# In the last attention round, the queries are made ahead of the expert sums, and the round's fill table is written anew

## The chip, the cores and the metric

The kernel runs on one core of a Trainium2 chip. The metric is the device time of one launch in microseconds (us): the median before is 1268.89 us over 3 runs (1267.88 to 1271.37). The engines are TensorE (PE in the profile, PEld its weight loads), VectorE (DVE), ScalarE (ACT), GpSimd (POOL) and SyncE (SP), which only issues DMAs here.

## The reference

Sixteen images become 49 tokens each, a class token and 128 text tokens are added, and the 178 tokens by 192 channels go through two attention layers and a mixture of four experts.

```
h = tokens(x)                                   # patch conv, wavelet branch, 3 depthwise convs, layernorm
h = concatenate([h, txt], axis=1)               # 16 x 178 x 192
h = h + attn(layernorm(h))                      # 12 heads of 16, own token masked, softmax, projection
h = h + ffn(layernorm(h))
...
def ffn(src):
    logits = gamma * zscore_last(Q @ K.T * scale)      # z-score over the 178 keys, per row
    attn = softmax(logits) @ V @ Wo.T + bo
    x = layernorm(src + attn) * g + b
    top-2 of softmax(x @ Wg.T + bg) over E = 4 experts -> combine
    y[e] = relu(x @ W1[e] + b1[e]) @ W2[e] + b2[e]     # 192 -> 768 -> 192
    return layernorm(x + sum_e combine[e] * y[e]) * g + b
```

## The kernel before, in words

The images are handled in 8 pairs. A pair passes three stages: attention 0 (the masked one), attention 1 (the one with z-scored logits) and the experts. The stages of different pairs run beside each other in rounds, `one_round(eng, a, b, nxt, m, fill)`: in one round attention 0 works on pair `a`, attention 1 on pair `b`, pair `nxt` is loaded and projected, and the experts work on pair `m`. Every engine has its own written-out program for a round (`pe_round`, `act_round`, `dve_round`, `sp_round`, `pool_round`), and the engines are tied together by semaphores. An engine works strictly in its written order: while it waits for one semaphore, nothing behind that wait can start.

The change is about the last round that has attention, `one_round(eng, None, PAIRS - 1, None, PAIRS - 2, FILL_B7)`: `a` and `nxt` are None, attention 1 works on pair 7 and the experts on pair 6. One more round follows with the experts of pair 7 alone.

Attention 1 in that round goes so. TensorE transposes the normed input (L749), projects queries (L757), keys (L757 again) and values (L765). VectorE first centres the input (`xbar`, L1268 to L1274), then closes the pair before it (`last.finish()`: the output layernorm of pair 5, L1166 to L726), splits the keys into three bf16 parts (L1185 to L1188, `ks`) and adds the value bias (L1195, L1199). From key Gram matrices (L878, L889, L895, L901, the last one called the ss sums here) and four ScalarE activations (L1086 to L1091) comes the factor `rem` of each query. VectorE multiplies the queries by it and splits them (`query`: L1303, L1185 to L1188, `qs`). SyncE stores `qs` to DRAM (L1527, `scr_q`) and loads it back in stacked form in six parts (L1534, `qst`); TensorE waits for all of them before the max pass (`pe_max_pass`: logits L792 and L798; VectorE takes the row maxima, `mx`, L1317). The maxima are split (L1323 to L1329), transposed (L825), cast on ScalarE (`mrows`, L1045) and sent by DMA into `qst` (L1545). Then comes the exp pass (`pe_exp_pass`: logits again, exponentials L1055, products with the values L851), the normalisation (L860, L1338, L1339), the projection (L866, L765) and the layernorm whose result is transposed at L966 for the experts of pair 7.

The expert work of pair 6 is cut into 50 steps, numbered 0 to 49. An even step `2u` is a group of five matmuls of 370 columns (L646, first layer of unit `u`); ScalarE's relu (`hid`, L681) follows. An odd step `2u+1` is the second layer of unit `u-1` (L668; printed as x6 in the profile, since each of three matmuls is two instructions). Four times VectorE adds an expert's sum to `acc` (`expert`, L696): it belongs to steps 13, 25, 37 and 48, and waits until TensorE has finished them; TensorE waits for the sum before it starts the next expert's second layer.

Where these steps stand among the attention work is set by the fill table: `moe.point("ss")` runs as many steps as the table has under "ss", and the three engines TensorE, ScalarE and VectorE call the same points in the same order. What the points have not used runs at `moe.rest()`. The names of points: "start", "norm", "query", "key", "value", "kc", "g", "u", "ss" in the front; ("max", 1) with a number for each of the six head pairs of the max pass; ("split", 1) after it; ("rows", 1) before the exp pass; ("exp", 1) with six numbers; ("out", 1), ("turn", 1), ("back", 1) in the output part. Points with a 0 are of attention 0 and are not called here.

Of the kernel before, what the change touches and what calls it, by code (L numbers as in the profile page):

```python
# [100 lines left out]
    "next query": 2,  # L101
}
FILL_B7 = {
    "start": 4, "norm": 1, "query": 3, "key": 4, "value": 0, "kc": 2, "g": 0, "u": 2, "ss": 14,
    ("max", 0): (0, 0, 0, 1, 1, 0), ("split", 0): 0, ("rows", 0): 0, ("exp", 0): (0, 0, 0, 0, 0, 0), ("out", 0): 1,
    ("max", 1): (0, 0, 0, 0, 0, 0), ("split", 1): 1, ("turn", 0): 1, ("back", 0): 2, ("rows", 1): 4,
    ("exp", 1): (1, 2, 0, 0, 0, 2), ("out", 1): 1, ("turn", 1): 2, ("back", 1): 0, "next turn": 0, "next norm": 3,
    "next query": 2,
}


# [15 lines left out]
def build(nc, a):  # L127
    ctx = ExitStack()
    with ctx:
        def sb(name, shape, dt=F32):  # L130
            return ctx.enter_context(nc.sbuf_tensor(name, shape, dt))
# [26 lines left out]
        rows = sb("rows", [128, NROW, D])  # L158
# [410 lines left out]
        def at(n, per, k):  # L569

            return n * per + k
# [167 lines left out]
        def moe_of(cls, eng, m, fill):  # L739
            return NoMoe() if m is None else cls(eng, m, fill)  # L740
# [163 lines left out]
        def pe_round(pe, a, b, nxt, m, fill):  # L904


            moe = moe_of(MoePe, pe, m, fill)
# [35 lines left out]
                pe.wait_ge(S["m_rows", 1], at(b, 1, 1))  # L943
            if a is not None:
                pe_out(pe, 0, a, moe)
                moe.point(("rows", 1))
                pe.wait_ge(S["pr_read", 0], at(a, 1, 1))
            if b is not None:
                pe_exp_pass(pe, 1, b, moe)
# [21 lines left out]
            if b is not None:  # L971
# [3 lines left out]
                for i in range(3):  # L975
                    o = 2 * E * i
                    for k, (x, plane) in enumerate(((x2T_hi, 0), (x2T_lo, 0), (x2T_hi, 1), (x2T_lo, 1))):
                        w = gate_b[:] if plane else gate_a[:].rearrange("p c e -> p (c e)")
                        ins = nc.tensor.matmul(PS[:, 2, o:o + (E if plane else 2 * E)], tile_cols(x, plane, i), w,  # L979
                                               start=(k == 0), stop=(k == 3), skip_group_check=True)  # L980
# [30 lines left out]
        def act_turn_in(act, s, r):  # L1011
            act.wait_ge(S["xT_psum", s], at(r, 1, 1))
            first = front(s, r)[0]
            src = PS[0:HC, first:first + 2, 0:XW]
            nc.scalar.copy(xT[s][:], src).then_inc(S["xT_ready", s], 1)  # L1015
# [53 lines left out]
        def act_out(act, s, r, moe):  # L1069
            moe.point(("turn", s))  # L1070
            act.wait_ge(S["oc_psum", s], at(r, 1, 1))
            nc.scalar.copy(oT[:], PS[0:HC, 0:2, 0:XW]).then_inc(S["oc_ready", s], 1)
            moe.point(("back", s))
# [20 lines left out]
        def act_round(act, a, b, nxt, m, fill):  # L1094
            moe = moe_of(MoeAct, act, m, fill)
            moe.point("start")
            if b is not None:
                act_turn_in(act, 1, b)
                moe.point("norm")
                act_query(act, 1, b)  # L1100
                moe.point("query")
                act_key(act, 1, b, a)
                moe.point("key")
                moe.point("value")
                act_deviation(act, b, moe)
                moe.point("ss")
            if a is not None:
                for u in range(HH):
                    moe.point(("max", 0), u)
                moe.point(("split", 0))  # L1110
                act_max_rows(act, 0, a)
                moe.point(("rows", 0))
                act_exp_pass(act, 0, a, moe)
                moe.point(("out", 0))
            if b is not None:
                for u in range(HH):
                    moe.point(("max", 1), u)
                moe.point(("split", 1))
                act_max_rows(act, 1, b)
            if a is not None:  # L1120
                act_out(act, 0, a, moe)
                moe.point(("rows", 1))
            if b is not None:
                act_exp_pass(act, 1, b, moe)
                moe.point(("out", 1))
            if b is not None:
                act_out(act, 1, b, moe)
            if nxt is not None:
                act_turn_in(act, 0, nxt)
                moe.point("next turn")  # L1130
                moe.point("next norm")
                act_query(act, 0, nxt)
                moe.point("next query")
                act_key(act, 0, nxt, b)
            moe.rest()
            if b is not None:
                act.wait_ge(S["x2T_psum"], at(b, 1, 1))
                nc.scalar.copy(x2T_hi[:], PS[:, 2:4, 0:XW]).then_inc(S["x2T_ready"], 1)
                act.wait_ge(S["gl_ready"], at(b, 1, 1))
                nc.scalar.activation(gl[:], gl[:], ACT.Exp).then_inc(S["ge_ready"], 1)  # L1140
# [241 lines left out]
        def dve_round(dve, a, b, nxt, m, fill):  # L1382
            moe = moe_of(MoeDve, dve, m, fill)
            last = moe_of(MoeDve, dve, None if m is None or isinstance(m, int) and m == 0 else m - 1, fill)
            moe.point("start")
            if b is not None:
                query = dve_front1(dve, b, a, moe, last)
                moe.point("ss")
            else:
                last.finish()  # L1390
            if a is not None:
                dve_max_pass(dve, 0, a, moe)
                moe.point(("split", 0))
            if b is not None:
                query(a)
            if a is not None:
                moe.point(("rows", 0))
# [6 lines left out]
            if a is not None:  # L1404
                dve_out(dve, 0, a, moe)
                norm1 = dve_norm1(dve, a)
                moe.point(("rows", 1))
            if b is not None:
                for u in range(HH):
                    moe.point(("exp", 1), u)  # L1410
# [333 lines left out]
```

## Time and profile before

| | |
|---|---|
| median of 3 runs | 1268.89 us |
| profiled execution | 1264.83 us, its span 1263.0 us |
| PE busy | 86% of the span |
| DVE, ACT, POOL busy | 54%, 32%, 4% |
| share of the last chain: PE, DVE, ACT, DMA | 64%, 13%, 4%, 2% |
| last attention round (first L646 of pair 6 to L966) | about 1088.4 to 1195.7 us of the span |

The times come from one profiled execution. Times of day in the rows are microseconds from the start of the span; a duration follows; a bracket tells how long the engine had been idle before and what ended that. Matmuls are pipelined, so listed durations of neighbours overlap; the price of a group is the distance between starts, which the chain of waits gives directly. "issue" in a bracket means that the profile names no releaser.

### The profile page before, as it was taken

Reading aid. Unit: us, or ns where it says so; the run is one execution under the profiler, and the core shown is the slowest. Engines: PE = TensorE matmul, PEld = TensorE weight load, DVE = VectorE, ACT = ScalarE, POOL = GpSimd, SP = SyncE. Lnnn points to the kernel's source line nnn. Section 1 sums busy time; section 2 is a strip of 40 time slices with the busy share of each in tenths; the row PEclk is TensorE's granted clock in tenths of the full one; section 3 lists DMA queues with packets and bytes.
Section 4 is the critical chain, followed back from the end, with each engine's and each line's share of the span. In section 5 each row is a group of like instructions: output and inputs, shape, how many; then the busy total and the mean of one; then the engine's idle time right before and its main releaser. Section 6 shows DMA issues by size and latency. Waiting matters only on the chain.

```text
span 1263.0 us, 18670 instructions
## 1 busy us (share of the span) xinstructions
PE 1090.2 (86%) x7404; PEld 798.9 (63%) x7404; DVE 679.8 (54%) x1874; ACT 398.4 (32%) x905; POOL 55.1 (4%) x90
## 2 busy tenths in 40 slices
PE   7798747786789999999999999999999999885895
PEld 4343424553467677767866785787578667773795
DVE  3367677344465457646746565576547643633332
ACT  1222222213322343334343334333343234221321
POOL 6011100000000000000000000000000000000000
PEclk9898867756689899989998999999899989895998
DMA  9000052422032204220530152033204220021000
GB/s 302 0 1 0 7 156 60 68 43 44 8 73 55 45 8 91 59 34 4 110 68 10 32 104 44 9 63 73 44 8 85 52 44 2 4 62 29 1 10 9
DMA packets 38478, 60.74 MB, mean 48 GB/s; under 512 B 5060, under 2 KB 30264, under 8 KB 37944
## 3 DMA queue, kind: packets, MB, share of 16 engines
q1 hardware_dynamic: 36112, 56.84, 21.0%
q10 hardware_dynamic: 2280, 2.72, 0.8%
q8 instruction: 58, 0.95, 0.3%
q14 instruction: 28, 0.23, 0.1%
HBM read 42.76 MB, written 16.34 MB: 47 GB/s over the span
## 4 chain that ended last, share of the span: by engine, by line
PE 64%; DVE 13%; ACT 4%; issue 3%; DMA 2%; SPq 1%; POOL 0%; DVEq 0%; ACTq 0%; POOLq 0%
PE PS L668 14%; PE PS L646 12%; PE PS L757 7%; DVE mx L1317 6%; PE PS L851 5%; PE PS L765 5%; PE PS L792 5%; PE PS L798 3%; PE PS L807 2%; PE PS L860 2%; PE PS L889 1%; DMA qst<-mrows 1%; PE PS L979 1%; ACT probs L1055 1%; DVE acc L696 1%
## 5 line engine op out<-in xcount | busy, mean ns | idle before, releaser
L668 PE MATMUL PS<-w,hid 128*128 128x192 f32 x1152 | 230.8, 338 | 3.0 <-DVE acc L696 1.8
L681 ACT ACTIVATE hid<-PS,b 128x370 f32<-128x370 f32 x192 | 109.1, 569 | 329.2 <-PE PS L646 327.5
L668 PEld LDWEIGHTS PS<-w,hid 128*128 128x128 f32 x1152 | 197.8, 196 | 12.8 <-issue 4.7
L1317 DVE TENSOR_REDUCE mx<-PS 128x2 f32<-128x356 f32 x288 | 128.4, 519 | 130.1 <-PE PS L792 102.5
L1055 ACT ACTIVATE probs<-PS 128x356 f32<-128x356 f32 x288 | 111.9, 484 | 30.2 <-PE PS L792 20.7
L646 PE MATMUL PS<-x2T_hi,w_hi 128*128 128x370 f32 x192 | 91.6, 477 | 0.0
L792 PE MATMUL PS<-kst,qst 96*128 96x178 bf16 x384 | 69.7, 278 | 17.5 <-issue 12.3
L757 PE MATMUL PS<-xT,w_at 96*96 96x370 f32 x192 | 78.3, 559 | 7.2 <-ACT xT L1015 3.5
L807 PE MATMUL PS<-masks,ident_bf 128*128 128x256 bf16 (+1 forms) x288 | 76.6, 266 | 0.0
L851 PE MATMUL PS<-probs,va 128*17 128x178 f32 x1536 | 69.2, 321 | 6.4 <-ACT probs L1055 6.4
L792 PE MATMUL PS<-qst,kst 99*128 99x178 bf16 x384 | 56.7, 251 | 17.8 <-DMA qst<-mrows 12.9
L646 PE MATMUL PS<-x2T_hi,w_lo 128*128 128x370 f32 x192 | 66.0, 344 | 0.0
L646 PE MATMUL PS<-x2T_hi,w_rest 128*128 128x370 f32 x192 | 65.9, 343 | 0.0
L646 PE MATMUL PS<-x2T_lo,w_hi 128*128 128x370 f32 x192 | 65.8, 343 | 0.0
L646 PE MATMUL PS<-x2T_lo,w_rest 128*128 128x370 f32 x192 | 65.5, 341 | 0.0
L757 PEld LDWEIGHTS PS<-xT,w_at 96*96 96x96 f32 x192 | 34.7, 189 | 41.1 <-issue 11.3
L1338 DVE RECIPROCAL rs<-PS 128x36 f32<-128x36 f32 x16 | 6.1, 382 | 100.1 <-PE PS L860 100.1
L792 PEld LDWEIGHTS PS<-kst,qst 96*128 96x128 bf16 x384 | 25.8, 104 | 53.4 <-DVE mx L1317 31.9
L851 PEld LDWEIGHTS PS<-probs,va 128*17 128x17 f32 x1536 | 40.5, 98 | 23.8 <-ACT probs L1055 9.3
L792 PEld LDWEIGHTS PS<-qst,kst 99*128 99x128 bf16 x384 | 28.1, 100 | 43.3 <-issue 26.1
L696 DVE SCALAR_TENSOR_TENSOR acc<-PS,comb,acc 128x192 f32<-128x192 f32 x72 | 25.5, 410 | 54.7 <-PE PS L668 54.7
L375 DVE SCALAR_TENSOR_TENSOR dwo<-pad_l,chan,dwo 96x441 f32<-96x441 f32 x48 | 38.1, 793 | 26.7 <-ACT cw L299 25.2
(226 smaller groups left out, 1723.8 us busy)
## 6 DMA issues: line engine op xcount, KB each, us to landing
qst<-scr_q SPq DMA_DIRECT2D x96, 144.0 KB, 4.8
scr_q<-qs SPq DMA_DIRECT2D x16, 432.0 KB, 3.3
scr_k<-ks SPq DMA_DIRECT2D x16, 432.0 KB, 3.7
kst<-scr_k SPq DMA_DIRECT2D x16, 432.0 KB, 5.0
kst<-scr_k SPq DMA_DIRECT2D x16, 288.0 KB, 5.9
cols<-in_x_cols SPq DMA_DIRECT2D x6, 392.0 KB, 13.4
w<-in_w SPq DMA_DIRECT2D x1, 2304.0 KB, 26.7
kst<-scr_k SPq DMA_DIRECT2D x16, 144.0 KB, 6.3
```

The source lines that it names most:

```text
L375: ch.link(nc.vector.scalar_tensor_tensor(out=out, in0=image_rows(PAD_OF[r][:, 0, :], tap_offset(t), n), scalar=col(C_DW + 18 * r + t), in1 ...
L646: ins = nc.tensor.matmul(PS[:, 4 + u % 2, 0:XN], w[:, f], x[:, plane, 0:XN], start=(k == 0), stop=(k == 4))
L668: ins = nc.tensor.matmul(tile_psum((6, 7), i), hid[u % 2][:, 128 * i:128 * i + 128], w2[:, u, :], start=(j == 0 and i != 1), stop=(j == FT ...
L681: nc.scalar.activation(hid[u % 2][:, 0:XN], PS[:, 4 + u % 2, 0:XN], ACT.Relu, bias=b1[:, u:u + 1]).then_inc(S["h_ready"], 1)
L696: ins = nc.vector.scalar_tensor_tensor(out=acc[:, i, :], in0=tile_psum((6, 7), i), scalar=comb[:, i, e:e + 1], in1=(acc if e else x2)[:, i ...
L757: ins = nc.tensor.matmul(PS[0:HC, banks[m], 0:XN], w_at[:, w, k, HC * m:HC * m + HC], x[:, k, 0:XN], start=(k == 0), stop=(k == 1))
L765: ins = nc.tensor.matmul(tile_psum(banks, i), tile_cols(x, k, i), w_at[:, w, k, :], start=(k == 0), stop=(k == 1))
L792: ins = nc.tensor.matmul(PS[:, bank, T * b:T * b + T], still[0:rows_, h, TP * b:TP * b + NTXT], move[0:rows_, h, TP * b:TP * b + T], start ...
L807: ins = nc.tensor.matmul(own, ident_bf[:], m.rearrange("p (b j) -> p b j", b=2), start=False, stop=True, skip_group_check=True)
L851: ins = nc.tensor.matmul(PS[32 * q:32 * q + VW, 3, T * b:T * b + T], va[s][:, 2 * i + b, h, :], pr, start=(i == 0), stop=(i == 1), skip_gr ...
L1055: nc.scalar.activation(probs[:, u % PROB_UNITS, bank, :], PS[:, bank, 0:T2], ACT.Exp)\
L1317: nc.vector.tensor_reduce(out, PS[:, g, 0:T2].rearrange("p (b j) -> p b j", b=2), AX.X, ALU.max)\
```

## The change

The fill table of this round, `FILL_B7`, gets new numbers. Summed over the points that are called, they give 39 steps before the rest in both kernels, but placed otherwise: before, 30 steps stand ahead of the max pass, none in it, 1 after it, none at ("rows", 1), 5 in the exp pass, 1 at "out", 2 at "turn", none at "back"; in the changed kernel 22, 4, 3, 4, 3, 0, 2 and 1. Of the 22, five stand in the front (three at "query", two at "key") and 17 at "ss".

The point ("rows", 1) is now called in rounds without `a` too. And in a round without `a`, VectorE calls `query` ahead of the point "ss" and no longer behind it. The other attention rounds have an `a` and keep their order; in the round after the last attention round the point ("rows", 1) runs one step of the table FILL that ran at the rest before, in the same order.

```diff
 FILL_B7 = {
-    "start": 4, "norm": 1, "query": 3, "key": 4, "value": 0, "kc": 2, "g": 0, "u": 2, "ss": 14,
-    ("max", 0): (0, 0, 0, 1, 1, 0), ("split", 0): 0, ("rows", 0): 0, ("exp", 0): (0, 0, 0, 0, 0, 0), ("out", 0): 1,
-    ("max", 1): (0, 0, 0, 0, 0, 0), ("split", 1): 1, ("turn", 0): 1, ("back", 0): 2, ("rows", 1): 4,
-    ("exp", 1): (1, 2, 0, 0, 0, 2), ("out", 1): 1, ("turn", 1): 2, ("back", 1): 0, "next turn": 0, "next norm": 3,
-    "next query": 2,
+    "start": 0, "norm": 0, "query": 3, "key": 2, "value": 0, "kc": 0, "g": 0, "u": 0, "ss": 17,
+    ("max", 0): (0, 0, 0, 0, 0, 0), ("split", 0): 0, ("rows", 0): 0, ("exp", 0): (0, 0, 0, 0, 0, 0), ("out", 0): 0,
+    ("max", 1): (0, 1, 1, 1, 1, 0), ("split", 1): 3, ("turn", 0): 0, ("back", 0): 0, ("rows", 1): 4,
+    ("exp", 1): (0, 1, 0, 1, 0, 1), ("out", 1): 0, ("turn", 1): 2, ("back", 1): 1, "next turn": 0, "next norm": 0,
+    "next query": 0,
 }
@@ pe_round @@
             if a is not None:
                 pe_out(pe, 0, a, moe)
-                moe.point(("rows", 1))
+            moe.point(("rows", 1))
+            if a is not None:
                 pe.wait_ge(S["pr_read", 0], at(a, 1, 1))
@@ act_round @@
                 act_out(act, 0, a, moe)
-                moe.point(("rows", 1))
+            moe.point(("rows", 1))
@@ dve_round @@
                 query = dve_front1(dve, b, a, moe, last)
+                if a is None:
+                    query(a)
                 moe.point("ss")
...
-            if b is not None:
+            if b is not None and a is not None:
                 query(a)
...
                 norm1 = dve_norm1(dve, a)
-                moe.point(("rows", 1))
+            moe.point(("rows", 1))
```

On VectorE, in the last attention round before, the expert sums (`acc`) of steps 13 and 25 stand ahead of the queries (`q`, `qs`), and the 18 row maxima (`mx`) stand in one piece:

```order
L696 SCALAR_TENSOR_TENSOR acc<-PS,comb,x_wide 128x192 x3
L1290 TENSOR_TENSOR probs<-PS,same_head 96x192 x2
L1297 TENSOR_TENSOR rem<-PS,q 96x4x178
L696 SCALAR_TENSOR_TENSOR acc<-PS,comb,acc 128x192 x3
L1303 SCALAR_TENSOR_TENSOR q<-q,chan,rem 96x4x178
L1185 CAST qs<-q 96x2x2x178
L1186 TENSOR_TENSOR rem<-q,qs 96x4x178
L1187 CAST qs<-rem 96x2x2x178
L1188 TENSOR_TENSOR qs<-rem,qs 96x2x2x178
L1317 TENSOR_REDUCE mx<-PS 128x2 x18
```

The same place of VectorE in the changed kernel, where these lines are numbered one higher:

```order
L1291 TENSOR_TENSOR probs<-PS,same_head 96x192 x2
L1298 TENSOR_TENSOR rem<-PS,q 96x4x178
L1304 SCALAR_TENSOR_TENSOR q<-q,chan,rem 96x4x178
L1186 CAST qs<-q 96x2x2x178
L1187 TENSOR_TENSOR rem<-q,qs 96x4x178
L1188 CAST qs<-rem 96x2x2x178
L1189 TENSOR_TENSOR qs<-rem,qs 96x2x2x178
L696 SCALAR_TENSOR_TENSOR acc<-PS,comb,x_wide 128x192 x3
L1318 TENSOR_REDUCE mx<-PS 128x2 x15
L696 SCALAR_TENSOR_TENSOR acc<-PS,comb,acc 128x192 x3
L1318 TENSOR_REDUCE mx<-PS 128x2 x3
```

Both sums moved behind the queries: the first stands before the maxima, the second between the fifteenth and the sixteenth of them.

On TensorE, at the end of the max pass of the same round before: the last logits (L792, L798), one step, and the transposes of the maxima (L825).

```order
L798 MATMUL PS<-kst,qst 64x178 x4
L792 MATMUL PS<-kst,qst 128x178 x4
L798 MATMUL PS<-kst,qst 64x178 x4
L646 MATMUL PS<-x2T_hi,w_hi 128x370
L646 MATMUL PS<-x2T_hi,w_lo 128x370
L646 MATMUL PS<-x2T_lo,w_hi 128x370
L646 MATMUL PS<-x2T_hi,w_rest 128x370
L646 MATMUL PS<-x2T_lo,w_rest 128x370
L825 MATMUL PS<-ident,mpart 36x128 x3
```

TensorE in the max pass of the changed kernel, from the second head pair's logits on:

```order
L792 MATMUL PS<-kst,qst 128x178 x4
L798 MATMUL PS<-kst,qst 64x178 x4
L646 MATMUL PS<-x2T_hi,w_hi 128x370
L646 MATMUL PS<-x2T_hi,w_lo 128x370
L646 MATMUL PS<-x2T_lo,w_hi 128x370
L646 MATMUL PS<-x2T_hi,w_rest 128x370
L646 MATMUL PS<-x2T_lo,w_rest 128x370
L792 MATMUL PS<-kst,qst 128x178 x4
L798 MATMUL PS<-kst,qst 64x178 x4
L668 MATMUL PS<-w,hid 128x192 x3
L792 MATMUL PS<-kst,qst 128x178 x4
```

A step now follows the logits of each of the head pairs 1 to 4; three more stand before L825 and four between L825 and the exp pass.

## Rows read from the trace of the kernel before

**Rows 1.** The page, busy time of TensorE: busy us (share), instructions.

```profile
PE 1090.2 (86%) x7404; PEld 798.9 (63%) x7404; DVE 679.8 (54%) x1874; ACT 398.4 (32%) x905; POOL 55.1 (4%) x90
```

**Rows 2.** Timeline of TensorE, 1145 to 1196 us: start, duration, instruction, idle before.

```profile
1145.00 0.75 PE L792 MATMUL PS<-kst,qst 96*128 96x178 bf16 x4 [12.26 <-issue]
...
1155.57 0.80 PE L825 MATMUL PS<-ident,mpart 128*36 128x128 f32 x3 [1.05 <-DVE mpart L1326]
1160.74 0.75 PE L792 MATMUL PS<-qst,kst 99*128 99x178 bf16 x4 [4.37 <-DMA qst<-mrows]
...
1161.86 2.29 PE L668 MATMUL PS<-w,hid 128*128 128x192 f32 x6
...
1181.53 2.22 PE L765 MATMUL PS<-w_at,oT 96*128 96x192 f32 x12 [0.88 <-ACT oT L1072]
...
1195.69 0.88 PE L966 MATMUL PS<-ident,x_wide 128*128 128x128 f32 x6
```

**Rows 3.** Timeline of VectorE, 1114 to 1153 us.

```profile
1114.96 0.90 DVE L1297 TENSOR_TENSOR rem<-PS,q 96x712 f32<-96x712 f32 x1 [1.54 <-PE PS L895]
1128.49 1.07 DVE L696 SCALAR_TENSOR_TENSOR acc<-PS,comb,acc 128x192 f32<-128x192 f32 x3 [12.64 <-PE PS L668]
1129.59 0.96 DVE L1303 SCALAR_TENSOR_TENSOR q<-q,chan,rem 96x712 f32<-96x712 f32 x1
...
1132.64 0.90 DVE L1188 TENSOR_TENSOR qs<-rem,qs 96x712 bf16<-96x712 f32 x1
1145.50 7.93 DVE L1317 TENSOR_REDUCE mx<-PS 128x2 f32<-128x356 f32 x18 [11.96 <-PE PS L792]
```

**Rows 4.** Timeline of ScalarE, the last activation before the queries.

```profile
1120.44 0.80 ACT L1091 ACTIVATE rem<-rem 96x712 f32<-96x712 f32 x1
```

**Rows 5.** Timeline of SyncE, the queries' store and loads.

```profile
1133.62 0.30 SPq L1527 DMA_DIRECT2D scr_q<-qs  x1
1136.91 2.63 SPq L1534 DMA_DIRECT2D qst<-scr_q  x6
```

**Rows 6.** Timeline of TensorE in the round's front, 1092 to 1122 us.

```profile
1092.98 0.82 PE L749 MATMUL PS<-ident,xn 128*96 128x128 f32 x6
...
1094.68 2.73 PE L757 MATMUL PS<-xT,w_at 96*96 96x370 f32 x8
...
1116.59 1.36 PE L901 MATMUL PS<-rem,same_head 96*96 96x356 f32 x4
...
1121.75 1.24 PE L668 MATMUL PS<-w,hid 128*128 128x192 f32 x6 [1.12 <-ACT hid L681]
```

**Rows 7.** Timeline of VectorE in the round's front, 1094 to 1110 us.

```profile
1094.66 0.68 DVE L1268 TENSOR_REDUCE xbar<-xT 96x4 f32<-96x512 f32 x1 [2.79 <-ACT xT L1015]
...
1103.11 0.76 DVE L726 TENSOR_TENSOR fin<-fin,h_fin 128x576 f32<-128x576 f32 x1
...
1108.84 0.71 DVE L1199 TENSOR_TENSOR va<-PS,rows 50x192 f32<-50x192 f32 x2
```

**Rows 8.** Chain of waits, two steps and a head pair's logits: start, us, what.

```profile
1125.66 0.98 PE PS L668 x6
1126.63 0.84 PE PS L646 x5
...
1172.08 0.41 PE PS L792 x4
1172.49 0.27 PE PS L798 x4
```

**Rows 9.** Stretches of 2 us, TensorE: length, PE busy (instructions), granted clock, DMA share, GB/s.

```profile
1030.00:1032.00 2.00, 1.90 (x11) 0.73 0.00 0
...
1084.00:1086.00 2.00, 0.12 (x1) 0.88 0.00 0
...
1120.00:1122.00 2.00, 0.88 (x5) 1.00 0.00 0
...
1164.00:1166.00 2.00, 2.00 (x17) 0.99 0.00 0
```

## The prediction

> **What bounds the kernel now.** I read the page's busy times first: TensorE is busy for 86% of the span [rows 1], so what can be won is its idle time, and what matters is where that lies. The chain of waits and TensorE's timeline of the last attention round show it. Ahead of the max pass TensorE stands still for 12.26 us; 1.05 us ahead of the transposes of the maxima, 4.37 us ahead of the exp pass [rows 2]. Then I followed the 12.26 us back. The six stacked query loads were issued from 1136.91, after a store at 1133.62 [rows 5], which waited for the last piece of the query split at 1132.64 + 0.90 = 1133.54 [rows 3]. The factor that the queries need was ready at 1120.44 + 0.80 = 1121.24 [rows 4], but VectorE took the queries up only at 1129.59: in its order an expert sum stood before them, for which it had waited 12.64 us [rows 3]. So 8.35 us of the standstill are order and not work. Also, after the long waits TensorE ran at half its rate: a second-layer step that costs 0.98 on the chain [rows 8] is listed with 2.29 us at 1161.86 [rows 2], against 1.24 us at 1121.75 [rows 6].
>
> **The change part by part.** All instructions stay; only places change. I place the changed round on the clock of the profiled execution.
>
> *The front.* Eight steps leave it (13 before "ss" to 5). One pair of steps costs 0.98 + 0.84 = 1.82 us on the chain [rows 8], so TensorE has 7.3 us less to do there. But VectorE then sets the pace. Before the input's sums at 1094.66 it had waited 2.79 us for the input, so it was free from 1091.87 [rows 7]. TensorE now transposes right after the gate matmuls and the gate's read, at about 1089.1 (the timeline has the last gate matmul at 1088.2 and the read ended at 1089.0), 0.8 us at full clock and up to 1.6 at half [rows 6], and ScalarE's copy takes 0.8, so VectorE starts at 1091.9, 2.76 earlier. Its work from 1094.66 to the end of `fin` at 1103.87 (9.2 us) moves as a block to end at 1101.1. The query and key projections cost 2.5 us each at full clock (a row of eight is listed with 2.73 [rows 6]); the first falls into the slow stretch after the gate, some 4.8 us, to 1096; two relu groups to 1097.7, keys to 1100.2, ScalarE's copy to 1101.1. So both releasers of the key split meet at 1101.1. A split takes 2.95 us (the queries' from 1130.59 to 1133.54, behind L1303 [rows 3]), the value bias 1.2 (its last piece of 0.71 in [rows 7], 0.5 for the first): 1105.3. From there before: the Gram product (1.87), mask (0.77), `u` product (1.45), `rem` (1.0), ss sums (1.3) make 6.4 us without steps between: ss sums end at 1111.8. Before they ended at 1116.59 + 1.36 = 1117.95 [rows 6]. **Gain 6.2 us.** Ends: if the clock stays low, see the slow rival (the end moves to 1124.7, a loss of 6.8); nothing lets it be better than 8.2 us, TensorE's removed steps plus the two waits of the block.
>
> *The queries.* ScalarE's four activations take 3.28 us (1117.96 to 1121.24), then VectorE starts after 0.05 and not after 8.35. Work and trip stay: 3.95 us for queries and split [rows 3], 11.46 us from the end of the split to the first logits at 1145.00 [rows 2, 5]. 1111.8 + 3.28 + 0.05 + 3.95 + 11.46 = 1130.5. **Gain 8.3 us.** SyncE has nothing in front of this store: key store and loads are now some 2.6 us earlier too. TensorE's 17 steps beside it: three run (2.8 us), then it waits for ScalarE, whose relus stand behind the four activations, as it waited 1.12 us before [rows 6]; fourteen take 7 x 1.82 = 12.7, plus 0.4 for the first expert sum: finished at 1128.7. So it waits about 1.8 us instead of 12.26. The expert sum behind the queries costs nothing, since VectorE is free from 1119.1 and the sum is asked for at about 1122.
>
> *Max pass to exp pass.* Before 15.74 us (1145.00 to 1160.74 [rows 2]) with one step inside; now eleven. VectorE needs 7.93 / 18 = 0.44 us for a maximum [rows 3]. TensorE needs 0.41 + 0.27 = 0.68 for the logits of a head pair [rows 8] and 0.84 to 0.98 for the step, 1.6 together, against 1.32 on VectorE: TensorE becomes the bound. Two head pairs, held by VectorE, to 1.9; four steps 3.7 and three more logits 2.0: 7.6. Now the second expert sum comes in between (1.1), then the last three maxima (1.3), the split of the maxima (2.0), 0.15: the transposes start 12.1 us after the pass, where it was 10.57. The three steps (2.8 us) hide behind this. From the transposes to the exp pass 5.17 us before, 4.9 with the transposes at full clock; the four steps (3.7) lie inside the DMA. Sum 17.1. **Loss 1.4 us.** Bounds: 15.4 if the step and the sum hid wholly, 25 at half clock (first rival).
>
> *Exp pass to L966.* Before 34.95 us (1160.74 to 1195.69 [rows 2]). Two steps fewer: 1.9. Full clock at its start saves the 1.25 us of the slow step and 0.5 of the logits. The step at "back" fills the wait of 0.88 ahead of L765 [rows 2]. The step missing at "out" opens 0.6. **Gain 4.0 us**, between 1.9 (only the steps) and 4.6.
>
> Sum: 6.2 + 8.3 - 1.4 + 4.0 = 17.1 us. The round of pair 7's experts that follows keeps its order and its length. I take 0.6 us off for hand-overs between engines that I rounded away in the two denser stages: 16.5 us. The profiled execution took 1264.83 us (span 1263.0) and would take 1248.3; the median of the runs is 1268.89, 0.3% above it. I take the 16.5 us from the median: 1252.4.
>
> **The clock.** The granted clock has two levels here. It fell at about 1085.5, in the stretch in which TensorE, after a wait, was busy for 0.12 of 2 us (a mean of 0.88 is half clock for the last 0.5 us), and it stayed at 1.00 where it was busy for 0.88 of 2 us between full work; it also fell, to a mean of 0.73, at 1030.9, where TensorE did logits in step with VectorE without steps between them [rows 9]. After the exp pass had begun at 1160.74, it came back at 1164.0 [rows 2, 9]. The new waits of the front are 1.0, 0.8 and 1.0 us, the one ahead of the max pass 1.8, with full work on both sides: nearer to the row that kept the clock. The Trainium skill has a rule against this (TensorE: Matmul & The Clock Gate, "A second HAM failure mode: psum-queue depth-cycling"): frequent micro-idles while a kernel cycles through PSUM banks make the clock switch back and forth between its levels. The fall at 1030.9 agrees with it. By that rule the max pass would still run cold, and the result would be the first rival's; by the row at 1120 it would run warm.
>
> **The rivals.**
> First: the clock falls in the 1.8 us or in the first logits. For: 1.8 us is near the waits before 1085.5, and the max pass of the round before fell so. Against: there, no step stood in the first three head pairs; now one follows the second. Price: four steps and the logits at half rate take 13.0 us where 7.6 stood, the four steps ahead of the exp pass 7 where 4.4 are covered: 8 us. Gain 8.5, 1260.4.
> Second: the front keeps its length, because VectorE's closing of the last pair and the slow clock decide it and not the removed steps. For: VectorE has 9.2 + 2.95 + 1.2 us to do in a row. Against: its wait of 2.79 us is plainly in the rows. Then 6.2 us are missing: gain 10.3, 1258.6.
> Third, slower: without the steps at "start" and "norm", TensorE's front is short work between waits, and the clock that fell at 1085.5 does not come back before the exp pass. Then front and steps cost double: ss sums at 1124.7, 17 steps of 1.54 to 1.94 us to 1155, the max pass as in the first rival and with three slow steps behind it, exp pass at 1182.3 instead of 1147.6. That is 34.7 us against the 17.1: 17.6 slower, 1286.5. It decides once the low clock lasts beyond about half of this stretch, some way into the 17 steps. Against: the query and key projections alone are solid work longer than that which brought it back at 1164.0.
> Fourth: no change. This needs the third to hold for just half of the stretch, or the expert steps to be the bound throughout; TensorE's standstill of 12.26 speaks against the latter.
>
> **How the numbers follow.** The forecast 0.62 (its own range 1250.3 to 1255.5, from the ends of the terms), first rival 0.17, second 0.10, third 0.04, no change 0.03; 0.04 for a larger gain, where all hand-overs turn out shorter. The range 1249.8 to 1261 takes in the first two rivals. A difference of about 0.3%, 3.8 us, is what a measurement of this kernel can tell from none: faster 0.93, within it 0.03, slower 0.04.
>
> **What would show it.** Measured from the last gate matmul: VectorE's first query instruction within 0.1 us of the end of ScalarE's last activation; store to first logits 11 to 12 us; TensorE's idle ahead of the max pass 1 to 3 us in place of 12.26; clock 1.00 from the first logits to the exp pass; idle ahead of the exp pass below 1.5 us; L966 about 90 us after the last gate matmul where it was 107. It is wrong if the clock is at half in the max pass (then by the first rival), if the key split starts later than 13 us after the last gate matmul (second), or if the wait ahead of the max pass stays above 5 us.

## The result, and the profile after

The changed kernel takes 1255.76 us in the median of 6 runs (1251.88 to 1258.30), the kernel before 1268.65 (1263.73 to 1271.37, 6 runs). The ratio is 0.9905, 95% interval 0.9885 to 0.9925: 0.75% to 1.15% faster. Timed again later, the same kernel had 0.9916 (0.9892 to 0.9941). The forecast of 1252.4 lay 3.4 us too low: within the stated range of 1249.8 to 1261, but just outside the forecast's own range of 1250.3 to 1255.5.

The profiled execution took 1251.88 us, its span is 1250.1 us. Its page reads for TensorE, columns as in [rows 1]:

```profile
PE 1086.6 (87%) x7404; PEld 795.4 (64%) x7404; DVE 680.3 (54%) x1874; ACT 398.3 (32%) x905; POOL 55.4 (4%) x90
```

The same number of instructions, and 12.9 us less span: 9.3 us of it are idle time of TensorE, 3.6 us busy time (1090.2 to 1086.6). TensorE's timeline of the last attention round, which answers to [rows 2]:

```profile
1089.14 4.88 PE L757 MATMUL PS<-xT,w_at 96*96 96x370 f32 x8 [0.88 <-ACT xT L1016]
...
1108.87 1.44 PE L901 MATMUL PS<-rem,same_head 96*96 96x356 f32 x4 [0.99 <-DVE rem L1298]
...
1129.28 0.47 PE L792 MATMUL PS<-kst,qst 96*128 96x178 bf16 x4 [2.22 <-issue]
...
1134.49 2.29 PE L668 MATMUL PS<-w,hid 128*128 128x192 f32 x6
...
1145.38 0.49 PE L825 MATMUL PS<-ident,mpart 128*36 128x128 f32 x3 [1.23 <-DVE mpart L1327]
1146.48 1.24 PE L668 MATMUL PS<-w,hid 128*128 128x192 f32 x6 [0.61 <-ACT mrows L1047]
...
1150.24 0.47 PE L792 MATMUL PS<-qst,kst 99*128 99x178 bf16 x4
```

The wait ahead of the max pass is 2.22 us in place of 12.26, and ahead of the exp pass there is none in place of 4.37. But between them stands a step of 2.29 us at 1134.49, the mark of the half clock.

VectorE's timeline answers to [rows 3]:

```profile
1107.92 0.90 DVE L1298 TENSOR_TENSOR rem<-PS,q 96x712 f32<-96x712 f32 x1 [1.54 <-PE PS L895]
1113.63 0.96 DVE L1304 SCALAR_TENSOR_TENSOR q<-q,chan,rem 96x712 f32<-96x712 f32 x1 [4.82 <-ACT rem L1092]
...
1116.68 0.90 DVE L1189 TENSOR_TENSOR qs<-rem,qs 96x712 bf16<-96x712 f32 x1
1119.14 1.07 DVE L696 SCALAR_TENSOR_TENSOR acc<-PS,comb,x_wide 128x192 f32<-128x192 f32 x3 [1.56 <-PE PS L668]
1129.70 2.71 DVE L1318 TENSOR_REDUCE mx<-PS 128x2 f32<-128x356 f32 x6 [9.50 <-PE PS L792]
1133.87 1.40 DVE L1318 TENSOR_REDUCE mx<-PS 128x2 f32<-128x356 f32 x3 [1.46 <-PE PS L792]
1137.12 1.40 DVE L1318 TENSOR_REDUCE mx<-PS 128x2 f32<-128x356 f32 x3 [1.85 <-PE PS L792]
```

The queries now wait for ScalarE alone and start as its last activation ends (1113.60). The maxima, one piece of 7.93 us before, are broken by waits of 1.46 and 1.85 us for TensorE. The stretches of 2 us around the max pass (columns as in [rows 9]):

```profile
1128.00:1130.00 2.00, 0.72 (x8) 1.00 0.00 0
1130.00:1132.00 2.00, 1.52 (x11) 0.77 0.00 0
1132.00:1134.00 2.00, 2.00 (x9) 0.50 0.00 0
...
1136.00:1138.00 2.00, 2.00 (x12) 0.52 0.00 0
1138.00:1140.00 2.00, 2.00 (x16) 1.00 0.04 8
```

The clock fell to its lower level (1.2 of 2.4 GHz) at about 1131.1, within the first logits, and was back at 1138.0.

For comparing kernels I cut the round at fixed instructions. Each number below is a difference of starts (ends for the last gate matmul and the ss sums) in one profiled execution of each kernel, in us. "Front" runs from the last gate matmul to the end of the ss sums, "trip" from there to the first logits of the max pass, then to L825, to the exp pass, and to L966; "tail" is from L966 to the end of the span. The labels are those of the experiments below. "ss 18" is a kernel with 18 steps at the point "ss"; a "spin" is a group of added matmuls whose result nobody uses and which only keep TensorE busy.

| | front | trip (TensorE's wait at its end) | to L825 | to exp pass | to L966 | sum | tail |
|---|---|---|---|---|---|---|---|
| before | 29.4 | 27.05 (12.26) | 10.57 | 5.17 | 34.95 | 107.1 | 67.3 |
| changed | 24.05 | 18.97 (2.22) | 16.10 | 4.86 | 31.60 | 95.6 | 68.3 |
| e11, changed again | 24.06 | 18.92 (2.17) | 16.13 | 4.87 | 31.61 | 95.6 | 68.2 |
| e1, queries only | 30.2 | 19.46 (4.67) | 10.51 | 5.17 | 35.65 | 101.0 | 68.2 |
| e2, table only | 24.0 | 25.60 (8.92) | 16.23 | 4.86 | 31.60 | 102.3 | 68.1 |
| e12, front only | 28.3 | 31.80 (12.93) | 10.58 | 5.17 | 35.97 | 111.8 | 68.3 |
| e8, start 4 | 29.4 | 18.74 (3.64) | 16.05 | 4.89 | 31.61 | 100.7 | 68.3 |
| e6, rows 0 | 24.0 | 18.94 (2.25) | 16.11 | 4.86 | 36.97 | 100.9 | 67.0 |
| e4, ss 18 | 24.1 | 19.42 (1.81) | 15.42 | 5.02 | 31.61 | 95.5 | 68.2 |
| e5, ss 19 | 24.0 | 19.01 (0.51) | 13.86 | 6.46 | 31.57 | 94.9 | 68.4 |
| e3, spin | 24.9 | 18.77 (0.0) | 13.18 | 4.86 | 31.60 | 93.3 | 68.2 |
| e9, two spins | 24.9 | 18.74 (0.0) | 13.18 | 4.86 | 31.60 | 93.3 | 65.6 |
| e10, pass spins | 28.9 | 18.87 (0.0) | 12.44 | 4.87 | 31.61 | 96.7 | 64.7 |
| e7, ss 19, gate spins | 27.85 | 18.84 (0.0) | 14.80 | 6.49 | 31.61 | 99.6 | 64.5 |

Of the 12.9 us between the two spans, 11.5 lie in the round. The last gate matmul itself came 2.3 us earlier in the changed kernel's profile (1086.26 against 1088.57), though no instruction before it has changed: in the profiled executions of the kernels that are alike up to there it lies anywhere from 1079.5 to 1092.8. The tail took 1.0 us back, though its instructions are those of before: the clock stood at 0.50 for 6.8 us there before and for 10.2 us in the changed kernel, and e1 and e12, whose tails are those of before too, have 68.2 and 68.3. So the round is the better measure of a single cause, and the timed medians of the whole. The round has a spread of its own: the front of e1 and the stretch from exp pass to L966 of e1 and e12 have the instructions of before, and took 0.8, 0.7 and 1.0 us longer.

### The profile page after: what moved, and what is told of

Its sections match the earlier page's. It is cut to its first block, busy times and chain, and to the rows that moved or that the text cites. A ratio compares the mean times of both kernels' runs of the same rounds, so it can differ in the third digit from the quotient of the medians.

```text
span 1250.1 us, 18671 instructions
## 1 busy us (share of the span) xinstructions
PE 1086.6 (87%) x7404; PEld 795.4 (64%) x7404; DVE 680.3 (54%) x1874; ACT 398.3 (32%) x905; POOL 55.4 (4%) x90
## 4 chain that ended last, share of the span: by engine, by line
PE 64%; DVE 14%; ACT 4%; DMA 2%; issue 2%; SPq 1%; POOL 0%; DVEq 0%; ACTq 0%; POOLq 0%
PE PS L668 15%; PE PS L646 12%; PE PS L757 7%; DVE mx L1318 6%; PE PS L851 5%; PE PS L765 5%; PE PS L792 5%; PE PS L798 3%; PE PS L807 2%; PE PS L860 2%; PE PS L889 1%; DMA qst<-mrows 1%; ACT probs L1056 1%; PE PS L980 1%; DVE acc L696 1%
## 5 line engine op out<-in xcount | busy, mean ns | idle before, releaser
L792 PE MATMUL PS<-kst,qst 96*128 96x178 bf16 x384 | 67.8, 273 | 8.8 <-issue 2.2
L792 PE MATMUL PS<-qst,kst 99*128 99x178 bf16 x384 | 56.0, 248 | 13.7 <-DMA qst<-mrows 8.6
L792 PEld LDWEIGHTS PS<-kst,qst 96*128 96x128 bf16 x384 | 26.2, 104 | 42.8 <-DVE mx L1318 30.0
L792 PEld LDWEIGHTS PS<-qst,kst 99*128 99x128 bf16 x384 | 27.4, 99 | 38.9 <-issue 21.0
```

Source lines behind the costliest of these rows:

```text
L792: ins = nc.tensor.matmul(PS[:, bank, T * b:T * b + T], still[0:rows_, h, TP * b:TP * b + NTXT], move[0:rows_, h, TP * b:TP * b + T], start ...
```

## The experiments

Each kernel was timed beside the kernel before. Given are medians, and the ratio to before with its 95% interval; what is said of a stretch comes from one profiled execution of each kernel.

**e1, only the queries ahead.** Fill table and point ("rows", 1) as before.

```diff
                 query = dve_front1(dve, b, a, moe, last)
+                if a is None:
+                    query(a)
                 moe.point("ss")
...
-            if b is not None:
+            if b is not None and a is not None:
                 query(a)
```

> Only VectorE's query call is moved ahead of the point ss; fill table and the point (rows, 1) as before. Theory (order on VectorE holds the trip through DRAM, one for one): the queries start 8.3 us earlier, the first logits 8.3 us earlier (TensorE's wait ahead of the max pass about 4 us in place of 12.26), the rest of the round as before: 7.5 to 9 us faster than before, about 1260.5. Rival (the table is what pays, the trip only moves the wait): under 4 us faster, and the wait turns up again ahead of the exp pass.

1259.61 us (12 runs), ratio 0.9960 (0.9935 to 0.9986). The trip is 7.6 us shorter, not 8.3: from the end of the split to the first logits it took 12.2 us here against 11.5 before. The front was 0.8 us longer, with the clock back at its upper level 5.4 us after the last gate matmul where it was 3.8 before, and the stretch behind the exp pass's start 0.7. The round is 6.2 us shorter: the theory's mechanism, a little under its numbers. The rival had the wait turn up again ahead of the exp pass; it is 4.37 us there, as before, so that part is refuted. The rival's size (under 4 us) lies inside the interval of the timed runs, which is 1.8 to 8.2 us. VectorE:

```profile
1124.36 0.96 DVE L1303 SCALAR_TENSOR_TENSOR q<-q,chan,rem 96x712 f32<-96x712 f32 x1 [5.42 <-ACT rem L1091]
...
1131.58 1.07 DVE L696 SCALAR_TENSOR_TENSOR acc<-PS,comb,acc 128x192 f32<-128x192 f32 x3 [3.27 <-PE PS L668]
```

The queries wait for ScalarE alone; TensorE waits 0.41 us for the expert sum behind them, as it did before.

**e2, only the table and the point ("rows", 1).** The queries stand behind "ss" as before.

> The new fill table with the point (rows, 1), but the queries behind the point ss as before. By the theory the front keeps its 5.3 us, but the queries now wait for the first expert sum, which in the changed kernel began 5.5 us after the queries did: they start 6.6 us later than in the changed kernel, TensorE waits about 9 us ahead of the max pass, and the low clock then lasts through the whole max pass with its steps inside. 1 to 5 us faster than before, 8 to 12 slower than the changed kernel. The rival (table pays alone) wants at least 9 us faster than before.

1262.52 us (12 runs), ratio 0.9979 (0.9953 to 1.0004). The round is 102.3 us, 4.8 less than before and 6.7 more than in the changed kernel. The trip is 6.6 us longer than there, as forecast; the round is less so than the 8 to 12 us expected. The rival (at least 9 us faster than before) falls, since the interval ends at 6 us; that the table alone gains at all is not resolved by the timed runs. The low clock lasted 13.6 us, from the long wait until 8.8 us into the pass, and not through the whole of it. Since the stretch to L825 is 16.23, the same as the changed kernel's, the long wait cost nothing beyond itself.

**e12, the front alone.** The kernel before with the five steps of "start" and "norm" put at "ss".

```diff
-    "start": 4, "norm": 1, "query": 3, "key": 4, "value": 0, "kc": 2, "g": 0, "u": 2, "ss": 14,
+    "start": 0, "norm": 0, "query": 3, "key": 4, "value": 0, "kc": 2, "g": 0, "u": 2, "ss": 19,
```

> The kernel before with the five steps of start and norm moved to ss (14 to 19), nothing else: the queries still stand behind the expert sum of step 25. Theory: the front shrinks by 5.3 us as in the changed kernel, but step 25 is now the 15th of ss and no longer the 10th, 4.6 us later behind the front's end, so the queries start only about 1 us earlier: 0 to 2 us faster than before. Rival (what leaves the front is gained wherever it goes): 4 to 6 us faster.

1269.19 us (12 runs), ratio 1.0043 (1.0016 to 1.0069): slower, which neither expectation had. The front shrank by 1.1 us and not by 5.3. Its clock was back at the upper level only 9.9 us after the last gate matmul, where it was 3.8 us before; how much of the missing 4.2 us that explains was not measured. The trip grew by 4.75, which was forecast. VectorE shows the sum of step 25 in front of the queries and what the wait for it costs:

```profile
1110.72 1.07 DVE L696 SCALAR_TENSOR_TENSOR acc<-PS,comb,x_wide 128x192 f32<-128x192 f32 x3 [5.01 <-PE PS L668]
1122.42 1.07 DVE L696 SCALAR_TENSOR_TENSOR acc<-PS,comb,acc 128x192 f32<-128x192 f32 x3 [10.63 <-PE PS L668]
1123.53 0.96 DVE L1303 SCALAR_TENSOR_TENSOR q<-q,chan,rem 96x712 f32<-96x712 f32 x1
```

So moving steps from the front to "ss" costs on the trip what it saves in the front, as long as the queries stand behind the sum of step 25. In e2, where only the sum of step 13 stood ahead of them, the round still gained 4.8 us.

**e8, four steps back at start.** "start": 4, "ss": 13, else the changed kernel.

> The changed kernel with four of the 17 steps of ss back at start. By theory the input is transposed about 4 us later, VectorE's block starts 2.9 us later, and the front is 27 us again in place of 24.05; TensorE then waits about 6 us ahead of the max pass, and the clock is low in all of it. 3 to 7 us slower than the changed kernel. Rival (the front is bound by TensorE's sum of work, so it only matters that 8 steps have left it): the front grows by all of 3.6 to 5 us. Second rival (the start was no bound): under 1 us slower.

1257.72 us (8 runs), ratio 0.9925 (0.9900 to 0.9950). The front is 29.4 us, 5.3 more than in the changed kernel and the whole of its gain; that is the first rival's size. The theory's cause gives part of it: VectorE's block started 3.7 us later after the last gate matmul (forecast 2.9), its key split 3.1 us later. The other 2.3 us came behind the key split, where the clock fell in the thin work of the front (stretches of 2 us):

```profile
1106.00:1108.00 2.00, 1.04 (x11) 1.00 0.46 112
1108.00:1110.00 2.00, 1.38 (x12) 0.90 0.37 109
1110.00:1112.00 2.00, 1.91 (x7) 0.50 0.87 194
```

In the timed runs the loss against the changed kernel is not resolved (intervals overlapping).

**e6, no steps at ("rows", 1).**

```diff
-    ... ("rows", 1): 4,
-    ("exp", 1): (0, 1, 0, 1, 0, 1), ...
+    ... ("rows", 1): 0,
+    ("exp", 1): (1, 2, 1, 1, 1, 1), ...
```

> The changed kernel without the four steps at (rows, 1); they run in the exp pass instead (1, 2, 1, 1, 1, 1). If those steps are hidden by the DMA that brings the maxima, TensorE stands 4.3 us idle again ahead of the exp pass and the exp pass grows by 3.7: 3.3 to 5 us slower than the changed kernel, more (up to 7) if the clock falls in that wait. Rival (the exp pass has room for four more steps beside ScalarE's exponentials): under 1.5 us slower.

1259.23 us (10 runs), ratio 0.9942 (0.9922 to 0.9962). The wait is back and the time to the exp pass does not change at all:

```profile
1148.01 0.49 PE L825 MATMUL PS<-ident,mpart 128*36 128x128 f32 x3 [1.19 <-DVE mpart L1327]
1152.87 0.75 PE L792 MATMUL PS<-qst,kst 99*128 99x178 bf16 x4 [4.36 <-DMA qst<-mrows]
```

The stretch behind grew from 31.60 to 36.97: four steps (3.7 us) and 1.7 more, with the clock at 0.50 when the exp pass began. The round is 5.3 us longer. The four steps at ("rows", 1) were hidden wholly.

**e3, TensorE kept busy ahead of the pass.** The added matmuls write a PSUM bank that is free then; the result does not use them.

```diff
                 moe.point("ss")
                 pe.wait_ge(S["ss_read"], at(b, 1, 1))
+                if a is None:
+                    for _ in range(12):
+                        nc.tensor.matmul(PS[:, 3, 0:XN], w1_hi[:, 0:128], x2T_hi[:, 0, 0:XN], start=True, stop=True, ...)
```

> The changed kernel with 12 added matmuls of 370 columns (0.17 us each, 2.1 us, into a PSUM bank that nobody reads then) where TensorE waited 2.22 us ahead of the max pass. If that wait is what lets the clock fall at 1131, the granted clock stays 1.00 through the max pass, the stretch from first logits to exp pass shrinks from 20.96 to about 17 us, and the kernel is 3 to 4.5 us faster than the changed one (14.5 to 17 faster than before). Rival (the short waits between logits make it fall, whatever stood before): the clock falls at the same place and the kernel is within 1 us of the changed one. Second rival: the added work is on the path, 0 to 1 us slower.

1253.20 us (7 runs), ratio 0.9900 (0.9862 to 0.9938). TensorE, then its clock, around the first logits:

```profile
1129.10 2.37 PE L813 MATMUL PS<-x2T_hi,w_hi 128*128 128x370 f32 x12
1131.42 0.48 PE L792 MATMUL PS<-kst,qst 96*128 96x178 bf16 x4
```

```profile
1129.00:1131.00 2.00, 2.00 (x14) 1.00 0.37 46
1131.00:1133.00 2.00, 1.63 (x15) 1.00 0.00 0
1133.00:1135.00 2.00, 1.90 (x17) 1.00 0.00 0
```

The clock stays at its upper level, and the stretch to L825 takes 13.18 us in place of 16.10: 2.9 us is what the fall had cost. In the round it is 2.3 us, less than the 3 to 4.5 forecast, since its front was 0.85 us longer: the clock came back 8.8 us after the last gate matmul, and 7.2 in the changed kernel. In the timed median the gain over the changed kernel is not resolved (0.9900 against 0.9905 and 0.9916, intervals overlapping).

**e4 and e5, real steps in that wait.** 18 steps at "ss" and ("max", 1) (0, 1, 1, 1, 0, 0); 19 and (0, 0, 0, 1, 1, 0).

> The changed kernel with one step more at the point ss (18) and one less in the max pass (head pair 4 has none). The step (0.85 us) runs in the wait of 2.22 us ahead of the max pass and leaves it. If the clock stays up by it, 3 to 5 us faster than the changed kernel; if the clock falls as before, about 1 to 1.5 us faster, since a step less runs at the low clock; if the max pass is bound by VectorE, no difference.

> The changed kernel with 19 steps at ss and two in the max pass (head pairs 3 and 4) instead of 17 and four. By theory the 19 steps fill the wait ahead of the max pass to about 0.4 us, so the clock stays at 1.00 as it did with the added matmuls of the run before, now without added work; the pass has two steps less. From the last gate matmul to L966 about 91.5 us where the changed kernel had 95.6: 4 us faster than it, 16 to 17 than before. Rival (the first three head pairs without a step between them let the clock fall, as in the round before): it falls inside the pass at the same place, and the stretch is 94 to 96 us.

e4: 1253.62 us (8 runs), 0.9906 (0.9874 to 0.9939); e5: 1253.60 us (6 runs), 0.9899 (0.9864 to 0.9934). e4 left a wait of 1.81 us, as its trip was 0.45 us longer, for a reason that was not looked for. The clock fell 1.4 us behind the first logits (1.8 in the changed kernel), came back, and fell a second time ahead of L825; the round was 0.1 us shorter, not the 1 to 1.5 forecast. e5 left 0.51 us, and the clock held for the first two head pairs, then fell in the logits that have no step between them:

```profile
1131.00:1133.00 2.00, 1.20 (x11) 1.00 0.00 0
1133.00:1135.00 2.00, 1.51 (x14) 1.00 0.00 0
1135.00:1137.00 2.00, 1.69 (x15) 0.95 0.00 0
1137.00:1139.00 2.00, 2.00 (x13) 0.50 0.03 8
```

It fell once more ahead of the exp pass (6.46 us where the others have 4.86). The rival was right for e5 that bare logits let the clock fall; the round took 94.9 us and not 91.5. Neither kernel is distinguishable from the changed one.

**e7, busy ahead of the gate too.** e5 with 11 added matmuls ahead of the last two gates.

```diff
+                if nxt is None:
+                    spin(11)
                 pe.wait_ge(S["x2T_lo"], at(b, 1, 1))
```

> e5's kernel with 11 added matmuls of 370 columns into an unread PSUM bank in the 2.04 us wait ahead of the gate matmuls, at the end of the last two attention rounds. Theory: that wait is what drops the clock at 1085 and again before the last expert round; held up, the gate matmuls, the first projections and the first expert steps run at full clock. The front is bound by VectorE and gains at most 1 us, the tail after L966 shrinks from 68.2 to about 64.5: 4 to 6 us faster than e5, about 1247. Rival (the gate matmuls of 4 and 8 columns themselves are too light and the clock falls in them anyway): within 1 us of e5. If the added matmuls push the gate matmuls back: 0.5 us slower.

1255.69 us (6 runs), 0.9898 (0.9862 to 0.9933), no better than e5. The tail is 3.9 us shorter, as forecast (64.5 for 68.4), and the clock did not fall around its gate. The front, which was to gain up to 1 us, lost 3.8:

```profile
1086.00:1088.00 2.00, 2.00 (x12) 0.72 0.00 0
1088.00:1090.00 2.00, 2.00 (x8) 0.50 0.00 0
1090.00:1092.00 2.00, 1.62 (x14) 0.93 0.00 0
1092.00:1094.00 2.00, 0.98 (x7) 0.93 0.00 0
1094.00:1096.00 2.00, 2.00 (x4) 0.50 0.00 0
...
1110.00:1112.00 2.00, 2.00 (x14) 0.69 0.53 143
```

The added matmuls did not hold the clock here. It fell at 1086.9, just as they began, so they ran at half rate and put the gate off by 1.1 us. It was back at 1090.3, for the gate matmuls, and fell again at 1093.7, 2.1 us behind the last of them, and the projections ran at half all the same; it was back at 1100.5 and fell a third time at 1110.8. The late return alone is not the whole price: in e3 it came as late (8.8 us after the last gate matmul, 8.9 here) and the front took 24.9 us. The rest of the 27.85 goes with the third fall.

**e9 and e10, the two places together.** e9: e3's matmuls ahead of the pass, and 11 ahead of the last gate alone. e10: 19 steps at "ss", two in the pass, three added matmuls behind the logits of head pairs 0 to 2, and the same 11.

```diff
                 pe_logits(pe, s, r, u, SROWS, qst[s], kst[s], S["s_used", s], S["s_psum", s])
+                if spins and u < 3:
+                    spin(3, 3)
```

> The changed kernel with 12 added matmuls (0.17 us each) ahead of the max pass and 11 in the wait ahead of the last gate matmuls, both into PSUM banks that nobody reads then. Theory: the two places are independent. From the last gate matmul to L966 93.3 us as with the first addition alone, and from L966 to the end 64.5 us as with the second alone, where the changed kernel had 95.6 and 68.2: 6 us faster than the changed kernel, about 18 to 19 faster than before (ratio 0.985). Rival: one of the two gives its gain back, as the added matmuls ahead of both gates did in the front; then 2 to 4 us faster than the changed kernel.

> As the kernel before this one in the tail, but with real work ahead of the max pass (19 steps at ss, two in the pass), and three added matmuls (0.5 us) behind the logits of each of the head pairs 0 to 2, where TensorE waits for VectorE's maxima. If the low clock of the 19-step kernel came from logits in step with VectorE, the clock now stays at 1.00, first logits to the transposes of the maxima take 12 us (13.9 there, 16.1 in the changed kernel), and the stretch to L966 is 91.5 us: the fastest of all, about 20 us faster than before. If it falls all the same, 94 to 95 us. The added matmuls cost up to 0.3 us each time if they stand in the way of the next logits.

e9: 1251.11 us (6 runs), 0.9893 (0.9852 to 0.9934); its round is 93.3 us as forecast and its tail 65.6 where 64.5 was forecast, the clock having fallen at 1182.6, at the first of the added matmuls ahead of the gate, and come back at 1186.0. e10: 1248.34 us (6 runs), 0.9871 (0.9838 to 0.9903), the fastest measured, and beside it the changed kernel had 1254.98 (12 runs). The intervals just overlap, so the order of the two is likely and not certain. In its profile the pass kept the clock and took 12.44 us to L825, 3.7 less than the changed kernel. e7 is the other half of this pair: it too had no wait ahead of the pass and the same steps, but no added matmuls between the logits, and its clock fell 3.2 us into the pass (14.80 us to L825). But the front of e10 went wrong:

```profile
1104.00:1106.00 2.00, 0.54 (x6) 1.00 0.28 73
1106.00:1108.00 2.00, 2.00 (x14) 0.69 0.55 148
1108.00:1110.00 2.00, 1.29 (x7) 0.50 0.58 118
```

Its front has the changed kernel's instructions one for one, and took 28.9 us and not 24.05. Nine of the profiles have this front. In six (changed, e2, e4, e5, e6, e11) the clock was back 7.2 to 7.3 us after the last gate matmul and the front took 24.0 us; in two (e3, e9) it was back after 8.8 us and the front took 24.9; in e10 it was back after 9.9 us, fell a second time at 1106.8, and the front took 28.9. The 24.05 is thus what the front takes while the clock holds; nothing in the kernel makes it hold.

**e11, the changed kernel once more.**

> The changed kernel once more, beside the others of this call. The stretch from the last gate matmul to L966 takes 95 to 96.5 us again, since its waits are set by order, and the clock falls within 1.5 us of the first logits; if the fall depends on chance and not on the wait and the logits, the stretch is 91 to 93 or 99 or more. Ratio to before 0.988 to 0.993.

1254.98 us (12 runs), 0.9916 (0.9892 to 0.9941). The round is 95.6 us again, and the clock fell 1.8 us behind the first logits in both.

## Why the prediction was right, and where it was not

*The order of the queries* was the core of it and held. From the end of the ss sums to the first logits 18.97 us were measured where the sum has 18.74; the gain is 8.1 us for 8.3. TensorE's wait there is 2.22 us, forecast 1.8. That the trip is set by VectorE's order is shown from both sides: e1 has this edit alone (trip 19.46, before 27.05), e2 everything else (25.60). The timed runs agree: the intervals of e1 and e2 both lie above the changed kernel's 0.9885 to 0.9925 (that of e1 just overlaps its later one, which ends at 0.9941).

*The front* was to end 23.2 us after the last gate matmul and ended after 24.05: a gain of 5.3 for 6.2. VectorE's block began 3.2 us after the last gate matmul (forecast 3.3). The key split came 0.44 us late, since it waited 0.55 us for the key projection; the other 0.4 us lie between the value bias and the end of the ss sums. The prediction miscounted the steps that leave the front: by the table it is 16 to 5, so eleven and not eight (13 to 5). The gain was worked out from VectorE's pace and not from this count, so only its upper bound (8.2 us) rests on it. The runs add a condition that the working had only in its slow rival: with four of the steps back and a fall of the clock (e8), or with that fall in the same code (e10), the front is 29 us and the gain is gone. How much of the 5.3 us is the steps alone is thus not shown; in e8 the key split is 3.1 us later with four of them back. The edits are also not independent: in e12 steps taken from the front, while the queries still stand behind step 25, were a loss.

*First logits to exp pass* is the term that failed: a loss of 1.4 us was forecast, 5.2 measured (20.96 us for 17.1). The step in question is the choice between two rows of the clock: I took the wait ahead of the pass to be nearer to the row that had kept it. It was nearer to the other. The clock at half in the max pass was one of the prediction's own signs that it is wrong, and it did occur; the total lay in the range all the same, because the other three terms nearly held and the range had room for the first two rivals. e3 puts 2.9 of the missing 3.8 us on the clock. Most of the remaining 0.9 is the price of steps: between logits they cost 1.05 and 1.17 us on the chain, not the 0.84 and 0.98 of neighbouring steps:

```profile
1139.52 1.17 PE PS L668 x6
```

The first rival thus had the right place and mechanism, and the wrong price: the clock fell at the first logits, but came back after 7 us instead of staying to the exp pass, 2.9 us and not 8. The steps inside the pass, which it counted as the load that gets dearer, are also full work; the clock returned at 1138.0, behind the first two of them. I had read its length off the pass before, where no step stood inside: there, and in e1 with the same bare pass, the clock stayed low for 27 and 20 us.

*Exp pass to L966* gained 3.35 us for 4.0, and by e1 and e12, which have the instructions of before here and took 35.65 and 35.97 us, it would be 4.05 or 4.4. e6 confirms the part on ("rows", 1): those steps were free, 5.3 us of the round hang on them, 3.7 as work and 1.7 through the clock.

Sum in the round: 5.3 + 8.1 - 5.2 + 3.35 = 11.5 us against 17.1; every term came out below its forecast. The second rival (the front keeps its length) did not occur in eight of the nine profiles with this front, and did in e10's. The third (half clock throughout, slower) never did. The rule of the Trainium skill that was set against this change (TensorE: Matmul & The Clock Gate, "A second HAM failure mode: psum-queue depth-cycling") was the better guide to whether the clock falls: e5 shows the fall inside logits that wait for PSUM banks with only 0.51 us of wait ahead of them. By its own way of putting it the clock goes back and forth, and it did. It is not the whole of it: in e3 the logits and steps are those of the changed kernel, and with the wait ahead of them filled the clock held.

What stays open: how often the front runs at 24 and how often at 29 us in the timed executions, which carry no trace. The spread of the changed kernel's runs, 1250.1 to 1259.2 us over 12, is of that size, but that does not tie it to the front: work ahead of the round moves the last gate matmul by up to 13 us between profiles, which is more.

## What to carry to other kernels

Where a long trip (a store and reload) hangs on one engine's result, look at what stands before that result in the engine's order, not at how busy the engine is: 7.6 us of the trip here were one call's place (e1). Fill work is worth what the wait covers at the point where it stands; steps that left the front lost their gain where a sum that came later by them stood ahead of the critical trip (e12). And when waits are filled, count the clock as a term of its own: a wait of 2.2 us left open ahead of short matmuls in step with another engine cost 2.9 us here (e3).

## What the runs showed of the hardware

Waits of 1.8 and 2.2 us ahead of the thin logits let the granted clock fall (e4, changed kernel); with the 2.2 us filled it held (e3), and with 0.5 us of wait and bare logits behind it fell 5 us later (e5). Three added matmuls of 370 columns behind each of the first three head pairs' logits held it (e10), though they are work for nothing; without them and equally without a wait it fell after 3.2 us (e7).

Keeping TensorE busy ahead of light work did not carry the clock over it: in e7 it fell as the added matmuls began, was back for the gate, fell again 2.1 us behind it and once more in the thin work, and the front was 3.8 us longer. The same 11 matmuls ahead of heavy work (the last expert round) made the tail 2.6 to 3.9 us shorter (e9, e10, e7).

The same instructions took 24.0, 24.9 or 28.9 us in the front, by where the clock fell and rose. A single profile of a stretch that is thin for TensorE is no measure of it.
